# Biases on the rows' last channel, shorter clearing, four first projections in four banks, four weights fetched earlier

## The chip, the core and the metric

The kernel runs on one core of a Trainium2 chip. The metric is the device time of one launch in microseconds (us). The kernel before took 3951.41 us, the median of three runs (3949.12 to 3953.07). Its profiled execution took 3948.97 us, of which 3947.2 us lie between its first and its last instruction.

## The reference

The input `u` is 4 x 1024 rows (4096 tokens) of 256 channels, all in f32. Layer 0 adds to it the output of a state-space recurrence and of a mixture of 64 experts (six of them per token). Layer 1, cut to what matters:

```
xn = layernorm(x)                       # over the 256 channels, no scale or shift
Q, K, V = xn @ Wq + bq, xn @ Wk + bk, xn @ Wv + bv       # each 1024 = 16 heads x 64
scores[t,h,i,j] = Q[t,h,i] * K[t,h,j] / 8,  j <= i       # a 64 x 64 triangle per token and head
attn[t,h,i] = sum_j softmax_j(scores)[i,j] * V[t,h,j]
x = x + attn @ Wo + bo + (silu(xn @ wg') * (xn @ wu')) @ wd'   # wg', wu', wd': int32 / 127
```

The normalised row `xn` is the only input of the five projections (`Wq`, `Wk`, `Wv`, `wg`, `wu`). Its channels sum to zero.

## The kernel before, in words

The program runs in stages, each a `Block` in which the five engines run their own instruction lists and after which they meet at a barrier. Before the change's first place come normalisation, routing and the recurrence.

**Experts** (`routed_experts`). 256 blocks of 128 rows run in 32 turns of 8. SyncE's queue (SP) fetches in `turn_in` three weights, four row blocks, five weights and four row blocks per turn. A weight is fetched only where the block's expert is another than the last one. TensorE computes, ScalarE and VectorE evaluate, GpSimd's queue scatters the results to DRAM.

**Combine** (`combine`). For each of 32 tiles of 128 tokens SP loads six expert rows per token (768 KB, a ring of five buffers), TensorE sums five of them and VectorE one (`own_choices`), VectorE measures and normalises, TensorE transposes, ScalarE copies and stores the transposed tile `xT`. Behind the first five loads SP also fetches all weights of layer 1: `Wq`, `Wk`, `Wv`, `Wo`, the three integer weights into `stage`, and the three biases, each repeated over 128 partitions, into `rest`. VectorE's `weights(step)`, spread over every second tile from tile 9 on, splits the f32 biases into three bf16 parts on rows of `k.bias` (rows 0, 64 and 96, picked by ones in `part_rows`) and converts the integer weights.

**Attention and feed-forward** (`attention_and_ffn`). A first `Block` clears buffers: GpSimd the tails of `q` and `m` and the four `pv` buffers, VectorE the six `s` buffers, each over its whole width of 2240 or 2496 elements. Then the second `Block` runs 32 tiles of 24 chunks each (`NCH`). One chunk holds four key rows of the score triangle or rectangle, up to 128x2048 elements. It goes through these engines:

- VectorE `products` multiplies q by k (at_s, L1195/L1196),
- GpSimd subtracts a bound of the maximum, `m` (at_s, L1276),
- ScalarE takes the exponential (at_s, L1355),
- TensorE adds it to the denominators (`sum_den`, at_den, L1509),
- VectorE `times_v` multiplies by v (at_pv), three chunks later,
- TensorE adds that to the numerators (`sum_num`, at_num).

Between the chunks, at fixed chunk numbers, stands the preparation of the next half tile. `project` computes one of six projections per tile, 128x512 each: K halves 0 and 1 of the next tile at chunks 4 and 8, V half 1 at chunk 11, Q half 0 of the next tile at 17, V half 0 at 19, Q half 1 at 22. All share one PSUM bank, `work`, so each waits until ScalarE has copied the one before out of it. Behind K come two scans of VectorE (L1419, L1422) and ScalarE's `keep_k`. Behind Q comes `keep_q` (three copies, the last is `fall`), and then GpSimd's `maxima`, whose first step (L1256) waits for `fall`. Behind V comes `keep_v`; `show_v` (at_vp, L1330) gives v to VectorE at chunks 1 and 17. On ScalarE, chunk 0 is followed by `keep_q` of Q half 1, then by the exponential of chunk 1, then by `show_v`.

The order on every engine is written out by hand, in the tables `prepare`, `KEEP_...`, `SCAN`, `MAXIMA_...`. Ahead of the loop stand five projections for tile 0.

Of the kernel before, what the change touches and what calls it, by code (L numbers as in the profile page):

```python
# [13 lines left out]
P = 128  # L14
# [16 lines left out]
HID = 768  # L31
# [605 lines left out]
def routed_experts(nc, k, io, scratch):  # L637
# [3 lines left out]
    with ExitStack() as ctx:  # L641
# [21 lines left out]
        w_in, x_in, y_out = ([a.sem(f"{s}{j}") for j in range(RING)] for s in ("w_in", "x_in", "y_out"))  # L663

# [10 lines left out]
        with nc.Block() as block:  # L675
# [183 lines left out]
            def _(sp):  # L859
# [25 lines left out]

                for i in range(TURNS):
                    turn_in(i)


def combine(nc, k, io, scratch):  # L890
    with ExitStack() as ctx:
# [10 lines left out]
        rest = a.sb("rest", [P, 3 * HC])  # L902
# [7 lines left out]
        members = lambda g: slice(g * GROUP, (g + 1) * GROUP)  # L910
        with nc.Block() as block:
# [11 lines left out]
            def _(dve):  # L923
# [8 lines left out]
                parts = k.bias[:].rearrange("p w n -> p (w n)")  # L932

                def weights(step):

                    if step == 0:
                        dve.wait_ge(w_in, 160)
                        c.mark(v.memset(k.keep_max[:], 0.0))
                        c.mark(v.memset(k.keep_min[:], 0.0))
                        c.mark(v.memset(k.part_rows[:], 0.0))  # L940
                        c.mark(v.tensor_copy(parts, rest[:]))
                    elif step == 1:
# [3 lines left out]
                        for row in (0, 64, 96):  # L946
                            c.mark(v.memset(k.part_rows[row:row + 1, :], 1.0))
# [18 lines left out]
                def normalise(g):  # L966
                    dve.wait_ge(pow_done, g + 1)
                    for n in range(g * GROUP, (g + 1) * GROUP):
                        v.tensor_scalar(xn[:, n, :], k.x[:, n, :], mv[:, n, 0:1], rstd[:, n:n + 1],
                                        ALU.subtract, ALU.mult).then_inc(xn_done, 1)  # L970
# [26 lines left out]
            def _(pe):  # L997
                for n in range(NT + AFTER):
# [40 lines left out]
            def _(sp):  # L1039
# [13 lines left out]
                for i, name in enumerate(("WqT", "WkT", "WvT")):  # L1053
                    sp.dma_start(k.wqkv[i][:], io[name].rearrange("(c p) n -> p c n", p=P)).then_inc(w_in, 16)
                for i, name in enumerate(("bq", "bk", "bv")):
# [647 lines left out]
```

## Time and profile before

| | |
|---|---|
| three runs, median | 3951.41 us |
| profiled execution | 3948.97 us, span 3947.2 us |
| TensorE matmul busy | 3548.3 us (90%) |
| GpSimd busy | 3342.6 us (85%) |
| VectorE busy | 3260.5 us (83%) |
| ScalarE busy | 1973.2 us (50%) |
| experts, from about 384 to 830 us | 446 us |
| combine, from about 834 to 958 us | 124 us |
| attention and feed-forward, from about 961 us | 2986 us |

Busy time is counted per engine; idle time of an engine is attributed to what it waited for. A matmul in f32 appears as two records. TensorE's clock has two levels, 1.2 and 2.4 GHz; a granted clock of 1.00 is the upper one and 0.50 the lower one. A share of 0.98 in a stretch is a mean over both.

### The profile page before, as it was taken

The numbers are of one execution on the slowest core, as the hardware profiler recorded it, in microseconds if no ns is written. First come the engines' busy times: TensorE is split into PE (matmuls) and PEld (weight loads), VectorE is DVE, ScalarE is ACT, GpSimd is POOL, SyncE is SP. The second block draws the span as 40 slices with busy tenths as digits, with TensorE's granted clock in tenths as the row PEclk, the third lists the DMA queues.
The fourth block names the chain that finished last, engine by engine and source line by source line (L and its number), as shares of the span: only waits on it lengthen the run. The fifth ranks groups of instructions, "written<-read, shape, count | busy, mean of one in ns | idle before, by whom it ended". The sixth has DMA issues, their size and how long they took to land.

```text
span 3947.2 us, 72250 instructions
## 1 busy us (share of the span) xinstructions
PE 3548.3 (90%) x25960; PEld 3110.3 (79%) x26155; DVE 3260.5 (83%) x3712; ACT 1973.2 (50%) x2535; POOL 3342.6 (85%) x1498
## 2 busy tenths in 40 slices
PE   5594999966899999999999999999999999999999
PEld 4253888854688888888888888888888888888888
DVE  8332666647798899999999999899999999999988
ACT  1010333334555555555555655565555566555555
POOL 1675665622899999999999999999999999999997
PEclk8797999987999999999999999999999999999999
DMA  9323565676000000000000000000000000000000
GB/s 380 125 104 123 172 184 178 188 266 236 3 5 5 5 5 5 5 5 5 5 6 6 8 5 5 5 5 5 5 5 6 5 7 5 6 7 5 5 5 5
DMA packets 110635, 209.30 MB, mean 53 GB/s; under 512 B 16610, under 2 KB 77282, under 8 KB 110306
## 3 DMA queue, kind: packets, MB, share of 16 engines
q1 hardware_dynamic: 84192, 140.90, 11.2%
q0 software_dynamic: 21504, 59.93, 4.0%
q8 instruction: 192, 3.15, 0.3%
q10 hardware_dynamic: 4608, 4.20, 0.3%
q14 instruction: 139, 1.12, 0.1%
HBM read 183.34 MB, written 107.74 MB: 74 GB/s over the span
## 4 chain that ended last, share of the span: by engine, by line
POOL 37%; PE 18%; issue 15%; DVE 3%; ACT 1%; another core or an unknown queue 0%; POOLq 0%; DVEq 0%; ACTq 0%
POOL at_s L1276 34%; PE at_num L1509 7%; PE at_den L1509 6%; PE at_work L1487 3%; POOL at_m L1261 1%; POOL at_fall L1258 1%; PE at_work L1497 1%; DVE at_pv L1195 1%; DVE at_k_low L1422 1%; PE at_misc L1541 1%; PE at_misc L1535 1%; ACT at_s L1355 1%; DVE at_s L1195 1%; POOL at_m L1256 0%; DVE at_k_top L1419 0%
## 5 line engine op out<-in xcount | busy, mean ns | idle before, releaser
L1276 POOL TENSOR_TENSOR at_s<-at_s,at_m 128x2048 f32<-128x2048 f32 (+7 forms) x768 | 2511.1, 3305 | 32.6 <-DVE at_s L1195 24.5
L1355 ACT ACTIVATE at_s<-at_s 128x2048 f32<-128x2048 f32 (+7 forms) x768 | 1080.5, 1418 | 610.2 <-POOL at_s L1276 609.9
L1509 PE MATMUL at_den<-k_ident,at_s 128*128 128x128 f32 x9216 | 1135.2, 273 | 53.3 <-ACT at_s L1355 53.2
L1509 PE MATMUL at_num<-k_ident,at_pv 128*128 128x128 f32 x9216 | 1141.7, 274 | 15.8 <-issue 5.6
L1509 PEld LDWEIGHTS at_num<-k_ident,at_pv 128*128 128x128 f32 x9216 | 1048.0, 142 | 92.1 <-issue 70.3
L1509 PEld LDWEIGHTS at_den<-k_ident,at_s 128*128 128x128 f32 x9216 | 1037.0, 141 | 85.0 <-ACT at_s L1355 61.0
L1196 DVE TENSOR_TENSOR at_pv<-at_s,at_vp 128x2048 f32<-128x2048 f32 (+7 forms) x512 | 688.7, 1345 | 226.2 <-ACT at_vp L1330 179.9
L1196 DVE TENSOR_TENSOR at_s<-at_q,at_kp 128x2048 f32<-128x2048 f32 (+7 forms) x512 | 687.9, 1344 | 13.7 <-ACT at_kp L1325 10.0
L1195 DVE TENSOR_TENSOR at_pv<-at_s,at_vp 128x2048 f32<-128x2048 f32 x256 | 582.7, 2276 | 0.0
L1195 DVE TENSOR_TENSOR at_s<-at_q,at_kp 128x2048 f32<-128x2048 f32 x256 | 580.1, 2266 | 0.0
L1487 PE MATMUL at_work<-k_region,at_xT 128*128 128x512 f32 x788 | 406.0, 641 | 105.9 <-ACT at_k_far L1296 82.2
L692 POOL DMA_INDIRECT picked<-moe_yo,moe_row x256 | 270.5, 1057 | 183.0 <-DVE moe_row L786 124.4
L1487 PEld LDWEIGHTS at_work<-k_region,at_xT 128*128 128x128 f32 x788 | 140.0, 198 | 219.5 <-issue 101.3
L140 POOL DMA_INDIRECT slot_x<-s_xn,s_slot x192 | 190.9, 994 | 140.2 <-DMA slot_x<-k_region 76.4
L714 PE MATMUL moe_gu<-moe_xT,moe_w 128*128 128x128 f32 x2048 | 276.5, 278 | 5.9 <-DVE moe_xT L836 5.7
L714 PEld LDWEIGHTS moe_gu<-moe_xT,moe_w 128*128 128x128 f32 x2048 | 250.5, 193 | 15.0 <-DVE moe_xT L836 13.8
L753 ACT ACTIVATE moe_gate<-moe_gu 128x128 f32<-128x128 f32 x256 | 71.0, 277 | 294.4 <-PE moe_gu L714 293.6
L1296 ACT COPY at_k_near<-at_work 128x256 f32<-128x256 f32 x66 | 24.6, 372 | 348.0 <-DVE at_k_low L1422 348.0
L1497 PE MATMUL at_work<-at_xT,k_region 128*128 128x128 f32 x1536 | 187.2, 275 | 0.0
L830 DVE TENSOR_TENSOR moe_hid<-moe_gate,moe_gu 128x128 f32<-128x128 f32 x256 | 73.2, 286 | 133.1 <-ACT moe_gate L753 128.3
L1497 PEld LDWEIGHTS at_work<-at_xT,k_region 128*128 128x128 f32 x1536 | 179.1, 192 | 0.0
L1256 POOL TENSOR_TENSOR at_m<-at_k_top,at_m 128x512 f32<-128x512 f32 x65 | 101.2, 1557 | 86.5 <-ACT at_fall L1310 85.7
(232 smaller groups left out, 3396.6 us busy)
## 6 DMA issues: line engine op xcount, KB each, us to landing
moe_w<-experts SPq DMA_DIRECT2D x256, 384.0 KB
slot_x<-k_region SPq DMA_DIRECT2D x16, 2144.0 KB, 25.4
moe_x<-slot_x SPq DMA_DIRECT2D x256, 134.0 KB, 2.3
cmb_y<-picked SPq DMA_DIRECT2D x32, 768.0 KB, 7.5
at_xT<-xT SPq DMA_DIRECT2D x33, 128.0 KB, 2.0
e_x<-u SPq DMA_DIRECT2D x4, 1024.0 KB, 9.3
picked<-moe_yo,moe_row POOLq DMA_INDIRECT x256, 3.1
xT<-cmb_xT ACTq DMA_DIRECT2D x32, 128.0 KB, 5.0
```

Of the source, the lines that this page charges most:

```text
L140: nc.gpsimd.indirect_dma_start(scratch["slot_x"], bass.IndirectOffsetOnAxis(ap=k.slot[:, n, j:j + 1], axis=0), k.xn[:, n, :], None).then_i ...
L692: pool.indirect_dma_start(scratch["picked"], bass.IndirectOffsetOnAxis(ap=row[i % 2][:, j:j + 1], axis=0), yo[j][:], None).then_inc(y_out[ ...
L714: ins = nc.tensor.matmul(gu[j % 2][:, s, :], w[j][:, (2 * s + c) * P:(2 * s + c + 1) * P], xT[j][:, c, :], start=(c == 0), stop=(c == DC - 1))
L830: nc.vector.tensor_tensor(hid[j][:], gate[j][:], gu[j % 2][:, 1, :], ALU.mult).then_inc(hid_ready, 1)
L1195: return nc.vector.tensor_tensor(by_row(out), by_row(other), keys, ALU.mult)
L1196: return nc.vector.tensor_tensor(out, other, keys, ALU.mult)
L1256: nc.gpsimd.tensor_tensor(rows(m[h]), turned(k_top), rows(m[h]), ALU.mult).then_inc(max_step, 1)
L1276: nc.gpsimd.tensor_tensor(part(s_slot, c), part(s_slot, c), by_query(m[unit_of(c)][:], c), ALU.subtract).then_inc(sub_done, 1)
L1355: nc.scalar.activation(part(s_slot, c), part(s_slot, c), ACT.Exp, scale=C ** -0.5).then_inc(exp_done, 1)
L1487: nc.tensor.matmul(work[:], xT[u][:, c, :], wqkv[which][:, c, cols], start=(c == 0), stop=False)
L1497: ins = nc.tensor.matmul(work[:, (2 * s + h) * P:(2 * s + h + 1) * P], w[:, c, tile * P:(tile + 1) * P], xT[u][:, c, :], start=(c == 0), s ...
L1509: ins = nc.tensor.matmul(dst[:, b * P:(b + 1) * P], buf[:, at:at + P], k.ident[:], start=(c in (0, NTRI) and x == 0 and b == 0), stop=Fals ...
```

## The change

The last channel (number 255) of every normalised row is set to 1.0 instead of its value. Since the channels sum to zero, the value there is minus the sum of the other 255, so the projections stay what they were if the last row of each weight is subtracted from all rows. The last row itself then becomes free and takes the bias (and zero for `wg` and `wu`).

- Projection: two f32 matmuls instead of two f32 matmuls and one bf16 matmul.
- Combine: GpSimd writes the ones once, VectorE normalises 255 columns, the `weights` steps subtract the last rows (`last`, `last_up`, fetched repeated over the partitions) from `Wq`, `Wk`, `Wv` (128x2048 each) and from the two integer weights (128x1536 each). SP waits for `shifted` and writes the three biases (4 KB each) over the last rows.
- `Wq`, `Wk`, `Wv` and `Wo` are fetched in the experts' stage, behind turns 6, 12, 18 and 24.
- The clearing `Block` is gone. Each engine clears at the head of the main `Block`, and of each `s` and `pv` buffer only the prefixes of its four rows (48 or 112 elements each).
- The first four projections go to four banks (`work`, `misc`, `num[1]`, `den[1]`), with no wait between them.

```diff
@@ routed_experts, SP @@
+                late = ((k.wqkv[0], "WqT"), (k.wqkv[1], "WkT"), (k.wqkv[2], "WvT"), (k.wo, "Wo"))
                 for i in range(TURNS):
                     turn_in(i)
+                    if i in (6, 12, 18, 24):
+                        dst, name = late[i // 6 - 1]
+                        sp.dma_start(dst[:], io[name].rearrange("(c p) n -> p c n", p=P)).then_inc(late_in, 16)
+                sp.wait_ge(late_in, 16 * len(late))
@@ combine @@
+                nc.gpsimd.memset(view(xn[:], [[D, NT]], D - 1), 1.0).then_inc(ones_set, 1)
...
-                        c.mark(v.memset(k.part_rows[:], 0.0))
-                        c.mark(v.tensor_copy(parts, rest[:]))
...
-                        c.mark(v.tensor_tensor(rest[:], rest[:], parts, ALU.subtract))
-                    elif step == 2:
-                        c(v.tensor_copy(parts[64:128, :], rest[64:128, :]))
-                    elif step == 3:
-                        c(v.tensor_tensor(rest[64:128, :], rest[64:128, :], parts[64:128, :], ALU.subtract))
-                    elif step == 4:
-                        c(v.tensor_copy(parts[96:128, :], rest[96:128, :]))
+                    if step < 3:
+                        w = k.wqkv[step]
+                        v.tensor_tensor(w[:], w[:], view(last[:], [[0, DC], [1, HC]], step * HC), ALU.subtract
+                                        ).then_inc(shifted, 1)
+                    elif step < 5:
+                        s = stage[step - 3][:].rearrange("p (c n) -> p c n", c=DC)
+                        c(v.tensor_tensor(s, s, view(last_up[:], [[0, DC], [1, HID]], (step - 3) * HID), ALU.subtract))
...
+                sp.wait_ge(shifted, 3)
+                for i, name in enumerate(("bq", "bk", "bv")):
+                    sp.dma_start(k.wqkv[i][P - 1:P, DC - 1, :], io[name].rearrange("(o n) -> o n", o=1)).then_inc(bias_in, 16)
@@ attention_and_ffn @@
-                for t in s_slot:
-                    nc.vector.memset(t[:], 0.0).then_inc(zeroed, 1)
+                for i in range(S_RING):
+                    v.memset(lead(s_slot, i), 0.0).then_inc(zeroed, 1)
...
-                        nc.tensor.matmul(work[:], xT[u][:, c, :], wqkv[which][:, c, cols], start=(c == 0), stop=False)
-                    nc.tensor.matmul(work[:], part_rows[:], bias[:, which, cols], start=False, stop=True
-                                     ).then_inc(work_done, 1)
+                        ins = nc.tensor.matmul(bank[:], xT[u][:, c, :], wqkv[which][:, c, cols], start=(c == 0),
+                                               stop=(c == DC - 1))
+                    ins.then_inc(work_done, 1)
...
                 project(0, 0, 1, 0)
+                project(0, 0, 1, 1, misc)
+                project(0, 0, 0, 0, num[1])
+                project(0, 0, 2, 0, den[1])
                 pe.wait_ge(k_out, 1)
-                project(0, 0, 1, 1)
-                pe.wait_ge(k_out, 2)
-                project(0, 0, 0, 0)
-                pe.wait_ge(q_out, 1)
-                project(0, 0, 2, 0)
+                project(0, 0, 0, 1)
                 pe.wait_ge(v_out, 1)
-                project(0, 0, 0, 1)
```

On TensorE, at the head of attention, stand before (L1487 is a projection's f32 matmul, L1488 its bias matmul, L1509 a sum of a chunk; at_work is the shared bank):

```order
L1487 MATMUL at_work<-k_region,at_xT 128x512 x2
L1488 MATMUL at_work<-k_bias,k_part_rows 128x512
L1487 MATMUL at_work<-k_region,at_xT 128x512 x2
L1488 MATMUL at_work<-k_bias,k_part_rows 128x512
L1487 MATMUL at_work<-k_region,at_xT 128x512 x2
L1488 MATMUL at_work<-k_bias,k_part_rows 128x512
L1487 MATMUL at_work<-k_region,at_xT 128x512 x2
L1488 MATMUL at_work<-k_bias,k_part_rows 128x512
L1487 MATMUL at_work<-k_region,at_xT 128x512 x2
L1488 MATMUL at_work<-k_bias,k_part_rows 128x512
L1509 MATMUL at_den<-k_ident,at_s 128x128 x20
```

And now, at the same place (L1492 and L1514 are the same two lines in the changed file):

```order
L1492 MATMUL at_work<-k_region,at_xT 128x512 x2
L1492 MATMUL at_misc<-k_region,at_xT 128x512 x2
L1492 MATMUL at_num<-k_region,at_xT 128x512 x2
L1492 MATMUL at_den<-k_region,at_xT 128x512 x2
L1492 MATMUL at_work<-k_region,at_xT 128x512 x2
L1514 MATMUL at_den<-k_ident,at_s 128x128 x20
```

Five bias matmuls are gone, and four of the five projections have a bank of their own. In the tile loop each projection loses its bias matmul in the same way and nothing else moves.

On SP's queue, at the head of combine, stand before (cmb_y is the ring of expert rows):

```order
L1044 DMA cmb_y<-picked 128x1536 x5
L1052 DMA cmb_bo<-bo 128x256
L1054 DMA k_region<-WqT 128x2x1024
L1054 DMA k_region<-WkT 128x2x1024
L1054 DMA k_region<-WvT 128x2x1024
L1056 DMA cmb_rest<-bq 128x1024
L1056 DMA cmb_rest<-bk 128x1024
L1056 DMA cmb_rest<-bv 128x1024
L1057 DMA k_region<-Wo 128x8x256
L1059 DMA cmb_stage<-wgT 128x2x768
L1059 DMA cmb_stage<-wuT 128x2x768
L1059 DMA cmb_stage<-wdT 128x6x256
```

And now, at the same place:

```order
L1049 DMA cmb_y<-picked 128x1536 x5
L1057 DMA cmb_bo<-bo 128x256
L1059 DMA cmb_last<-WqT 128x1024
L1059 DMA cmb_last<-WkT 128x1024
L1059 DMA cmb_last<-WvT 128x1024
L1061 DMA cmb_last_up<-wgT 128x768
L1061 DMA cmb_last_up<-wuT 128x768
L1063 DMA cmb_stage<-wgT 128x2x768
L1063 DMA cmb_stage<-wuT 128x2x768
L1063 DMA cmb_stage<-wdT 128x6x256
L1049 DMA cmb_y<-picked 128x1536 x8
```

Four weights and three repeated biases have left this place, five repeated last rows have come.

On SP's queue behind the experts' turn 6 stands now (before, the second row is not there; turns 12, 18 and 24 have `WkT`, `WvT` and `Wo` in its place):

```order
L868 DMA moe_x<-slot_x 128x268 x4
L892 DMA k_region<-WqT 128x2x1024
L873 TENSOR_LOAD c_fetch
L873 ISA x2
L874 ISA
L874 DMA moe_w<-experts 128x768
```

The weight has come between the last row blocks of one turn and the first expert weight of the next.

## Rows read from the trace of the kernel before

**Rows 1.** Windows: us, busy us (instructions) per engine, granted clock, DMA share, GB/s.
```profile
384.00:830.00 446.00, 410.97 (x3044) 364.35 (x3042) 293.19 (x1145) 164.88 (x509) 270.47 (x256) 1.00 0.59 180
...
834.40:958.50 124.10, 87.84 (x384) 72.37 (x384) 78.10 (x184) 61.78 (x192) 15.01 (x16) 0.83 0.92 334
...
863.10:876.90 13.80, 4.83 (x16) 4.04 (x17) 2.56 (x7) 0.94 (x4) 0.00 (x0) 0.57 1.03 406
...
1103.70:3846.90 2743.20, 2616.38 (x20275) 2358.53 (x20453) 2529.77 (x1771) 1591.10 (x1620) 2657.72 (x931) 0.99 0.02 6
```
**Rows 2.** Windows of two single tiles, the same columns (PE, PEld, DVE, ACT, POOL).
```profile
1195.00:1286.80 91.80, 87.48 (x677) 78.67 (x682) 84.31 (x60) 53.15 (x55) 88.49 (x32) 0.98 0.02 6
...
2385.20:2475.40 90.20, 86.14 (x678) 78.17 (x683) 84.40 (x60) 52.95 (x55) 88.73 (x33) 1.00 0.02 6
```
**Rows 3.** Groups of GpSimd, 1103.7 to 3846.9 us: busy, mean ns, idle before and releasers.
```profile
L1276 POOL TENSOR_TENSOR at_s<-at_s,at_m 128x768 f32<-128x768 f32 (+1 forms) x721 | 2356.1, 3302 | 30.3 <-DVE at_s L1195 23.7 <-POOL at_m L1261 3.6 <-DVE at_s L1196 1.3
L1256 POOL TENSOR_TENSOR at_m<-at_k_top,at_m 128x512 f32<-128x512 f32 x60 | 93.5, 1558 | 55.2 <-ACT at_fall L1310 54.5
```
**Rows 4.** Timeline of GpSimd: start, us, what, idle before it and its releaser.
```profile
1926.45 1.54 POOL L1256 TENSOR_TENSOR at_m<-at_k_top,at_m 128x512 f32<-128x512 f32 x1 [0.82 <-ACT at_fall L1310]
...
1970.81 4.57 POOL L1276 TENSOR_TENSOR at_s<-at_s,at_m 128x2048 f32<-128x2048 f32 x1 [0.65 <-DVE at_s L1195]
...
2001.32 1.56 POOL L1256 TENSOR_TENSOR at_m<-at_k_top,at_m 128x512 f32<-128x512 f32 x1 [1.48 <-ACT at_fall L1310]
...
2464.76 8.64 POOL L1276 TENSOR_TENSOR at_s<-at_s,at_m 128x2048 f32<-128x2048 f32 x3 [0.17 <-DVE at_s L1196]
2473.89 1.54 POOL L1256 TENSOR_TENSOR at_m<-at_k_top,at_m 128x512 f32<-128x512 f32 x1 [0.49 <-ACT at_fall L1310]
```
**Rows 5.** Timeline of ScalarE and VectorE around the hand-over of Q half 1 and v.
```profile
1924.80 0.58 ACT L1306 COPY at_q<-at_work 128x512 f32<-128x512 f32 x1 [1.30 <-remote]
...
2473.68 0.43 ACT L1355 ACTIVATE at_s<-at_s 128x256 f32<-128x256 f32 x1
...
1927.25 2.29 DVE L1196 TENSOR_TENSOR at_pv<-at_s,at_vp 128x2048 f32<-128x2048 f32 x1 [5.61 <-ACT at_vp L1330]
```
**Rows 6.** Timeline of TensorE, matmuls (PE) and weight loads (PEld), around two projections.
```profile
1940.34 1.88 PE L1487 MATMUL at_work<-k_region,at_xT 128*128 128x512 f32 x4
1942.27 1.04 PE L1509 MATMUL at_num<-k_ident,at_pv 128*128 128x128 f32 x8
...
1969.28 2.43 PE L1487 MATMUL at_work<-k_region,at_xT 128*128 128x512 f32 x4 [2.41 <-ACT at_k_far L1296]
...
1941.20 0.19 PEld L1487 LDWEIGHTS at_work<-k_region,at_xT 128*128 128x128 f32 x1 [0.24 <-issue]
1941.63 0.10 PEld L1488 LDWEIGHTS at_work<-k_bias,k_part_rows 128*128 128x128 bf16 x1 [0.24 <-issue]
```
**Rows 7.** Timeline of four engines at the start of attention.
```profile
973.90 2.14 DVE L1211 MEMSET at_s<- 128x2496 f32 x1 [0.47 <-issue]
...
976.53 0.83 SPq L1223 DMA_DIRECT2D at_xT<-xT  x2
...
978.54 3.78 PE L1487 MATMUL at_work<-k_region,at_xT 128*128 128x512 f32 x4 [21.36 <-DMA at_xT<-xT]
...
983.92 1.19 DVE L1422 TENSOR_TENSOR_SCAN at_k_low<-k_region,at_work 128x512 f32<-128x512 f32 x1
...
961.07 0.24 POOL L1203 MEMSET at_q<- 128x64 f32 x2 [7.14 <-POOLq L911]
...
1004.89 8.60 POOL L1276 TENSOR_TENSOR at_s<-at_s,at_m 128x2048 f32<-128x2048 f32 x3 [1.43 <-DVE at_s L1196]
```
**Rows 8.** Timeline of TensorE in combine, its first sum behind the weights' transfers.
```profile
872.07 8.17 PE L1004 MATMUL cmb_acc<-cmb_y,cmb_diag 128*128 128x256 f32 x30 [19.61 <-DMA cmb_y<-picked]
```
**Rows 9.** Timeline in the experts: SP's queue, then TensorE.
```profile
593.64 1.77 SPq L867 DMA_DIRECT2D moe_x<-slot_x  x4
...
597.81 0.43 PE L705 MATMUL moe_tr<-k_ident,moe_x 128*128 128x128 f32 x2 [0.73 <-DMA moe_x<-slot_x]
```

More of the change, by code:

```diff
@@ L901, in combine @@
         stage = [a.sb(f"stage{i}", [P, DC * HID], I32) for i in range(3)]
-        rest = a.sb("rest", [P, 3 * HC])
+        last = a.sb("last", [P, 3, HC])
+        last_up = a.sb("last_up", [P, 2, HID], I32)
+        shifted, bias_in, ones_set = a.sem("shifted"), a.sem("bias_in"), a.sem("ones_set")
         tr = [a.ps(f"tr{j}", [P, DC, P]) for j in range(2)]
@@ L1283, in tile @@
                             gated(t)
+                for x in (q[0], q[1], m[0], m[1]):
+                    nc.gpsimd.memset(x[:, HALF:QL], 0.0).then_inc(padded, 1)
+                for i in range(PV_RING):
+                    nc.gpsimd.memset(lead(pv_slot, i), 0.0).then_inc(padded, 1)
+                pool.wait_ge(padded, 4 + PV_RING)
                 for step in range(3):
@@ L1290, in _, with keep_k @@
             def _(act):
-                def keep_k(t, u, half):
+                def keep_k(t, u, half, bank=work):
                     act.wait_ge(scanned, t * 4 + (half * 2 + 2))
@@ L1305, in keep_q, with keep_v @@
                     wait(act, mult_done, past)
-                    nc.scalar.copy(q[h][:, 0:HALF], work[:])
+                    nc.scalar.copy(q[h][:, 0:HALF], bank[:])
                     wait(act, sub_done, past)
-                    nc.scalar.activation(m[h][:, 0:HALF], work[:], ACT.Relu)
+                    nc.scalar.activation(m[h][:, 0:HALF], bank[:], ACT.Relu)
                     wait(act, max_step, n * 3)
-                    nc.scalar.activation(fall[:], work[:], ACT.Relu, scale=-1.0).then_inc(q_out, 1)
-                def keep_v(n, use):
+                    nc.scalar.activation(fall[:], bank[:], ACT.Relu, scale=-1.0).then_inc(q_out, 1)
+                def keep_v(n, use, bank=work):
                     act.wait_ge(work_done, use)
                     wait(act, vp_ready, n)
-                    nc.scalar.copy(vv[:], work[:]).then_inc(v_out, 1)
+                    nc.scalar.copy(vv[:], bank[:]).then_inc(v_out, 1)
                 def keep_up(t, r, use):
@@ L1410, in times_v, with scan @@
                     multiply(part(pv_slot, c), part(s_slot, c), by_key(vp[:], c), c).then_inc(pv_done, 1)
-                def scan(t, half, step, use):
+                def scan(t, half, step, use, bank=work):
                     flat = lambda x: x[:].rearrange("p h c -> p (h c)")
@@ L1468, in tile @@
                             output(t - 1)
+                for i in range(S_RING):
+                    v.memset(lead(s_slot, i), 0.0).then_inc(zeroed, 1)
                 for half in range(2):
                     for step in range(2):
-                        scan(0, half, step, half + 1)
+                        scan(0, half, step, half + 1, (work, misc)[half])
+                dve.wait_ge(zeroed, S_RING)
+                dve.wait_ge(padded, 4 + PV_RING)
                 tile_loop(dve, tile)
@@ L1481, in _, with project @@
             def _(pe):
-                def project(t, u, which, half):
+                def project(t, u, which, half, bank=work):
                     pe.wait_ge(xT_in[u], 8 * (t - u) + 16)
@@ L1630, in lay_out_shared @@
     k.wqkv = [wq, wk, wv]
-    k.bias, k.part_rows = a.sb("bias", [P, 3, HC], BF16), a.sb("part_rows", [P, P], BF16)
 def build(nc, io, scratch):
```

47 lines of the change are left out of this document (19 added, 28 removed).

## The prediction, written before the changed kernel ran

> **What bounds the kernel now.** I read the windows first, to see in which stage the time lies. Of 3947.2 us, 2743.2 are thirty tiles of attention, 91.44 us each [rows 1]. There GpSimd is busy for 2657.7 us, 88.6 per tile, and TensorE for 2616.4. So GpSimd is the busiest engine, and 88.6 us is a floor that no part of this change moves. The groups of GpSimd [rows 3] tell what stands above the floor: its first maximum step waited 54.5 us for ScalarE's `fall` copy and its subtractions 25.0 us for VectorE's products, together with small waits 85 us in thirty tiles.
>
> The two single tiles show that there are two kinds [rows 2]. One takes 91.8 us at a mean clock of 0.98, the other 90.2 us at 1.00. A mean of 0.98 is one stretch at the lower level. Of the thirty windows from 1103.7 us on, 22 are of the first kind and 8 of the second. GpSimd works 88.5 and 88.7 us in them, so the 1.6 us between them is idle time of GpSimd that TensorE's clock causes.
>
> The timeline of GpSimd shows where it waits [rows 4]. In a tile with the drop: 1.48 us for `fall` of Q half 0 (at 2001.32), 0.82 for `fall` of Q half 1 (at 1926.45) and 0.65 for VectorE at chunk 12 (at 1970.81). In a tile without: 0.49 for Q half 1, none for Q half 0.
>
> Following these back gives a ring. ScalarE waited 1.30 us for the projection Q half 1 ("remote" is its PSUM bank) and then shows v. VectorE starts on it at 1927.25 after 5.61 us idle [rows 5], and works without a pause until its K scan, behind which V half 1 starts at 1969.28, after 2.41 us in which TensorE idled [rows 6]. From there TensorE works without a pause through V half 1, Q half 0, V half 0 to Q half 1. So per tile VectorE's part and TensorE's part follow each other, and four bias matmuls lie in TensorE's part. The other two (K halves) lie beside VectorE's part and only lengthen TensorE's idle time.
>
> **Part 1, the bias matmuls (33 us gained).** Four records of a projection stand 0.43 us apart (weight loads at 1941.20 and 1941.63), so they take 1.72. From the first of them to the next sum are 1942.27 - 1940.34 = 1.93 us [rows 6]. The bias matmul is the rest, 0.21 us at the upper clock, 0.42 at the lower.
>
> - Tile with a drop: four of them leave the ring, one at the lower clock (V half 1 took 2.43 instead of 1.88 us and begins at the drop). 3 x 0.21 + 0.42 = 1.05, I take 1.0. Such a tile goes to 90.8. GpSimd does not stop this: of its 3.3 us of waiting (91.8 - 88.5), the two for `fall` shrink.
> - Tile without: the four give 0.85, but ScalarE has the exponential of chunk 1 ahead of `show_v`. It began at 2473.68 [rows 5], and GpSimd had finished chunk 1 at 2464.76 + 8.64 = 2473.40 [rows 4]. So only 0.28 us can be gained there before ScalarE waits for GpSimd instead. Behind that GpSimd's own path is late next. I take 0.25; the tile goes to 89.9. The bounds are 0.25 and 0.49, what GpSimd waits for `fall`.
>
> How many tiles keep the drop is not in the rows. The idle time that goes with it, 2.41 us, becomes about 0.2 longer (K half 1 loses its bias too), but the tile gets another length and the drop has been missing in tiles with the same wait. I take half. Then a tile is 90.35 on the mean, 1.09 less than 91.44, and for 30.5 tiles (tile 0 has no such waits, the last has half) 33 us. All tiles with the drop: 0.64 x 30.5 = 20. None: 1.54 x 30.5 = 47. The share as today (22 of 30): 90.56, 27.
>
> **Part 2, the clearing (15.4 us gained).** The last clearing of VectorE ended at 976.04 and SP issued the first `xT` load at 976.53, while the stage had begun at 961.07 on GpSimd [rows 7]. Without the barrier the load is issued at about 961.1. The small clearings are hidden: six on VectorE, at most a fifth of the elements of the old ones, before its first scan, which waits for the load (978.54 - 976.53 = 2.0 us) and the first projection (3.8 us); GpSimd's before its first maximum, much later still.
>
> **Part 3, four banks (11 us gained).** From the first projection at 978.54 to GpSimd's first subtraction at 1004.89 are 26.35 us [rows 7]. The projections ran at the lower clock (four records in 3.78 us, 0.86 apart). In a row, without biases, four take 13.8 us at that clock and 0.2 to end, so V is there at 992.5 in the old times. Copying v and showing k take 0.6 each and the product 2.3 [rows 5], the hand-over 0.2: the subtraction starts at 996.2, 8.7 us earlier. If the clock rises after K half 0, V is there at about 987.3, but then the K scans and ScalarE's copies are late next: scan of K half 0 at 982.1, of half 1 until 986.7 (four scans of 1.19 us [rows 7]), ScalarE's two copies of k in 0.7 (an estimate, half as wide as the 0.6 us copies), three of q in 1.6, v and k in 1.1, product 2.3 and hand-overs, giving 993.4, which is 11.5 earlier. In combine TensorE resumed at 872.07 [rows 8], and the mean clock of 863.1 to 876.9 was 0.57 [rows 1], which is 1.9 us at the upper level: it rose 2.9 us after the work resumed. So I expect it to rise during the first projections, and take 11; bounds 8.6 and 12. The Trainium skill, "TensorE: Matmul & The Clock Gate", section "Part 1: The HAM clock gate (the "warmup" mystery)", says that the throttled state is the default and activity releases it; by that rule, to which this row agrees, the value is 11.5, and if it did not hold here, 8.7.
>
> **Part 4, combine (9 us gained).** The stage is bound by its transfers: 0.92 busy, 334 GB/s over 124 us, with VectorE at 78 us of 124 [rows 1]. TensorE waited 19.61 us for the sixth load behind the weights [rows 8]. By the shapes of the queue's rows, out go 4 x 1024 + 3 x 512 = 5632 KB, in come 3 x 512 + 2 x 384 = 2304 KB. The difference is 3328 KB or 3.41 MB: 8.4 us at the 406 GB/s of the wait, 10.2 at the stage's 334. I take 9, with bounds 7 and 12. The Trainium skill, "DMA: Bandwidth & Descriptors", section "Specifications", gives a limit of about 358 GB/s from HBM per core; the row of 406 is above it, and by the page the term would be 9.5. VectorE's new steps are three of 128x2048 (2.29 each by the product of that size [rows 5]) and two of 128x1536 (an estimate of 1.7 each), 10.3 us in place of as many steps over 3072 columns, so they are costed at nothing; they stand beside the loads. If that cover were gone they cost part of their 10.3, which the lower bound of 7 allows for. TensorE's new wait for the ones ends before its first data. SP's wait for `shifted` stands behind the last load; queued behind it are the last three stores, and the shifts are done by tile 13.
>
> **Part 5, the experts (7 us lost).** Four transfers of 1.05 MB, 2.6 us each at 406 GB/s, come between turns. Behind each stand the next three expert weights and the row blocks, whose first was issued at 593.64 and for which TensorE already waited 0.73 us at 597.81 [rows 9]. The transfer engines are busy 0.59 of this stage [rows 1], so some of each is absorbed in the 7 us between. I take 1.75 each, 7 in all; bounds 0, and 4 x (2.6 + 0.5 for issuing) = 12.4.
>
> **Sum.** 33 + 15.4 + 11 + 9 - 7 = 61.4. The profiled execution took 3948.97 us: 3887.6. It is 2.4 below the median of the runs, by which the sum gives 3890. I predict 3889.
>
> **Rivals.**
> - The drop comes in every tile, because TensorE idles longer before V half 1. For it: the idle time grows. Against: 8 of 30 tiles escape with about the same wait. Part 1 gives 20: 3902.
> - The drop is gone, since the tile's length changes. Part 1 gives 47: 3875.
> - GpSimd is the bound and the loop gains nothing. For it: 88.6 of 91.4 us busy, by far the fullest. Against: its waits end with ScalarE, and those with TensorE. Part 1 gives 0: 3922.
> - Slower: with less work TensorE falls to the lower clock more than once per tile, also in the pause around chunk 8. The price of a drop is 1.6 us per tile. Parts 2 to 5 give 28.4 us, so it decides from two drops in every tile (90.8 + 1.6 = 92.4, 0.96 x 30.5 = 29 lost), and three give 3999. Against: TensorE works 87.5 of 91.8 us. The Trainium skill, "TensorE: Matmul & The Clock Gate", section "HAM oscillation — how this bites in real kernels", says a loop with pauses for data can be throttled anew in each round; the trace agrees that one does so in 22 tiles of 30.
>
> **How the numbers follow.** Forecast 56%, drop in every tile 17%, drop gone 15%, no gain in the loop 9%, slower 2%, and 1% that the parts cancel. The forecast's own terms, with all at their bounds, span 3874 to 3903. The range reaches to the two rivals beside it and their bounds: 3864 to 3917. A change of 0.2% (7.9 us) is about what a measurement of this kernel tells from none. Faster by more 0.97, within it 0.01, slower 0.02.
>
> **What the changed profile would show.** Tiles of 89.9 and 90.8 us, at clocks of 1.00 and 0.98; GpSimd's wait for `fall` down from 54.5 to below 25 us in thirty tiles. First `xT` load within 1 us of the stage's start; the first subtraction about 17 us behind the load, not 28. TensorE's long wait in combine near 11 us instead of 19.6. In the experts four waits for row blocks 1 to 3 us longer than now. Wrong would be: tiles still at 91.4, or an experts' stage longer by over 12 us.

## The result: 3863 us, 2.2% less than before

The changed kernel takes 3862.6 us (median of four runs, 3861.58 to 3867.46), the kernel before beside it 3951.64 (3949.12 to 3953.07). The ratio is 0.9778, with a 95% interval of 0.9761 to 0.9795. That is 89 us gained, where 61 were forecast, and 1.4 us below the end of the range (3864). The direction, the ring of engines and the two parts at the start of attention were right. The step that failed is the bound on what a tile without a drop of the clock can gain: 0.25 us was forecast, 0.84 came. Combine's term was too small as well.

The profiled execution took 3861.88 us. The head of its page:

```profile
span 3860.1 us, 72041 instructions
PE 3497.0 (91%) x25958; PEld 3084.9 (80%) x25958; DVE 3241.8 (84%) x3708; ACT 1971.6 (51%) x2535; POOL 3336.4 (86%) x1499
```

GpSimd's own work is nearly what it was (3336 against 3343 us; the 6 us are its shorter clearing). Of the 87.1 us by which the span is shorter, 81 are waiting of GpSimd. They fall into four stretches, each read between two marks that both traces have:

| stretch, us | before | after | gain | forecast |
|---|---|---|---|---|
| start to the first load of expert rows (end of the experts) | 834.39 | 837.46 | -3.1 | -7 |
| from there to the start of the attention stage (combine) | 126.7 | 114.1 | 12.6 | 9 |
| stage start to GpSimd's first subtraction | 43.8 | 17.3 | 26.5 | 26.4 |
| first subtraction to the end (the loop) | 2942.3 | 2891.3 | 51.0 | 33 |

So the start of attention came out as worked out, and the miss is the loop (18 us), combine (3.6) and the experts (3.9).

Windows of the changed kernel, to be held beside [rows 1, 2]: us, then busy us (instructions) of PE, PEld, DVE, ACT and POOL, the granted clock, DMA share and GB/s. The last three are consecutive tiles, cut where GpSimd begins chunk 1.

```profile
384.00:833.00 449.00, 413.45 (x3040) 364.93 (x3038) 293.26 (x1146) 165.10 (x509) 270.89 (x256) 0.99 0.61 188
837.50:951.50 114.00, 85.39 (x384) 69.76 (x384) 75.39 (x180) 61.80 (x192) 15.53 (x17) 0.89 0.93 339
880.00:920.00 40.00, 35.31 (x168) 28.69 (x167) 38.39 (x83) 27.18 (x84) 8.20 (x6) 1.00 1.01 359
...
2409.40:2499.70 90.30, 86.12 (x674) 78.03 (x673) 84.34 (x59) 53.03 (x54) 88.58 (x33) 0.98 0.02 6
2499.70:2589.70 90.00, 85.82 (x682) 78.13 (x681) 84.08 (x59) 53.02 (x54) 88.63 (x33) 1.00 0.02 6
2589.70:2679.00 89.30, 85.12 (x678) 77.54 (x677) 84.08 (x59) 53.02 (x54) 88.61 (x33) 1.00 0.02 6
```

This pattern of three repeats through most of the loop: a tile with the clock's drop (0.98 on the mean), the one behind it, which still pays for it at its head, and a clean one of 89.3. The second to the thirty-first tile, from 1057.5 to 3752.6 us, take 89.84 us each, against 91.41 before (1093.5 to 3835.9). 11 of these 30 have a drop, before 22 of 30. All counts of drops below are of the same thirty tiles.

The groups of GpSimd in the loop (busy, mean ns | idle before and releasers) answer to [rows 3]:

```profile
L1272 POOL TENSOR_TENSOR at_s<-at_s,at_m 128x768 f32<-128x768 f32 (+1 forms) x720 | 2354.4, 3305 | 22.6 <-DVE at_s L1203 14.3 <-DVE at_s L1204 3.0 <-POOL at_m L1257 2.0
L1252 POOL TENSOR_TENSOR at_m<-at_k_top,at_m 128x512 f32<-128x512 f32 x60 | 93.6, 1560 | 15.8 <-ACT at_fall L1311 14.1
```

The wait for `fall` went from 54.5 to 14.1 us (below 25 was expected) and that for VectorE from 25.0 to 17.3.

Here is the start of attention in the timeline of the changed kernel (start, us, engine, line, what, idle before it), to be held beside [rows 7]:

```profile
951.56 0.84 SPq L1219 DMA_DIRECT2D at_xT<-xT  x2
951.67 2.06 DVE L1472 MEMSET at_s<- 128x192 f32 x6 [4.68 <-PEq L920]
953.60 3.78 PE L1492 MATMUL at_work<-k_region,at_xT 128*128 128x512 f32 x4 [5.94 <-DMA at_xT<-xT]
957.18 2.54 PE L1492 MATMUL at_misc<-k_region,at_xT 128*128 128x512 f32 x4
959.56 1.88 PE L1492 MATMUL at_num<-k_region,at_xT 128*128 128x512 f32 x4
961.28 1.88 PE L1492 MATMUL at_den<-k_region,at_xT 128*128 128x512 f32 x4
...
964.43 1.52 POOL L1252 TENSOR_TENSOR at_m<-at_k_top,at_m 128x512 f32<-128x512 f32 x1 [11.23 <-ACT at_fall L1311]
...
968.85 4.50 POOL L1272 TENSOR_TENSOR at_s<-at_s,at_m 128x2048 f32<-128x2048 f32 x1
```

The load goes out at the stage's start. The projections follow each other without a gap; the first ran at the lower clock (3.78 us), the second partly, the others at the upper (1.88). The first subtraction stands 17.3 us behind the load.

### The profile page after: what moved, and what is told of

Its sections match the earlier page's. It is cut to its first block, busy times and chain, and to the rows that moved or that the text cites. A ratio compares the mean times of both kernels' runs of the same rounds, so it can differ in the third digit from the quotient of the medians.

```text
span 3860.1 us, 72041 instructions
## 1 busy us (share of the span) xinstructions
PE 3497.0 (91%) x25958; PEld 3084.9 (80%) x25958; DVE 3241.8 (84%) x3708; ACT 1971.6 (51%) x2535; POOL 3336.4 (86%) x1499
## 4 chain that ended last, share of the span: by engine, by line
PE 53%; DVE 13%; issue 8%; ACT 1%; DVEq 0%; POOL 0%; ACTq 0%; DMA 0%; POOLq 0%
PE at_num L1514 20%; PE at_den L1514 18%; PE at_work L1492 8%; DVE at_s L1203 5%; PE at_work L1502 4%; DVE at_pv L1203 4%; PE at_misc L1540 2%; DVE at_k_low L1423 2%; PE at_misc L1546 1%; DVE at_k_top L1420 1%; DVE at_pv L1204 1%; ACT at_k_far L1297 0%; ACT at_s L1356 0%; DVEq L49 0%; DVEq L1407 0%
## 5 line engine op out<-in xcount | busy, mean ns | idle before, releaser
L1514 PE MATMUL at_den<-k_ident,at_s 128*128 128x128 f32 x9216 | 1136.1, 273 | 64.0 <-ACT at_s L1356 63.9
L1514 PE MATMUL at_num<-k_ident,at_pv 128*128 128x128 f32 x9216 | 1141.1, 274 | 0.5 <-DVE at_pv L1204 0.5
L1514 PEld LDWEIGHTS at_num<-k_ident,at_pv 128*128 128x128 f32 x9216 | 1047.1, 142 | 107.0 <-issue 96.2
L1514 PEld LDWEIGHTS at_den<-k_ident,at_s 128*128 128x128 f32 x9216 | 1037.9, 141 | 95.8 <-ACT at_s L1356 59.5
L1492 PE MATMUL at_work<-k_region,at_xT 128*128 128x512 f32 x776 | 378.7, 611 | 87.3 <-ACT at_k_far L1297 81.4
L1492 PEld LDWEIGHTS at_work<-k_region,at_xT 128*128 128x128 f32 x776 | 133.9, 192 | 190.2 <-issue 94.9
L706 PE MATMUL moe_tr<-k_ident,moe_x 128*128 128x128 f32 x512 | 101.0, 280 | 62.9 <-DMA moe_x<-slot_x 62.6
```

The lines of the kernel that those rows point to most:

```text
L706: ins = nc.tensor.transpose(tr[j % 2][:, c, :], xr[:, j, c * P:(c + 1) * P], k.ident[:])
L1492: ins = nc.tensor.matmul(bank[:], xT[u][:, c, :], wqkv[which][:, c, cols], start=(c == 0), stop=(c == DC - 1))
L1514: ins = nc.tensor.matmul(dst[:, b * P:(b + 1) * P], buf[:, at:at + P], k.ident[:], start=(c in (0, NTRI) and x == 0 and b == 0), stop=Fals ...
```

## The experiments

Each was run with the kernel before on the same chip; the ratios are against that. The stretches of e1 to e8 are compared with the changed kernel's trace. Times are compared with the changed kernel's median, which is of another round: the kernel before took 3951.6 us beside it, 3946.6 beside e1 to e4, 3951.2 beside e5 to e8 and 3947.3 beside e9 to e11. So a difference of up to 5 us between two medians tells nothing without a trace.

**e1_add_k and e2_add_vq: which bias matmuls were worth something.** A bf16 matmul on zeros takes the place of the bias matmul in the loop, in e1 only behind the two K projections, in e2 only behind the V and Q projections.

```
+                    if more:      # e1: which == 1 (K); e2: which != 1 (V, Q)
+                        ins = nc.tensor.matmul(bank[:], zb[:, 0:P], zb[:], start=False, stop=True)
```

> The changed kernel with one bf16 128x512 matmul of zeros put back into the two K projections of each tile (62 in all, 0.21 us each, 13 us of TensorE). Theory A (ring: TensorE's part runs from V half 1 to Q half 1, VectorE's part from v to the K scan): the K projections lie beside VectorE's part, so only TensorE's idle time before V half 1 shrinks, from 2.6 to about 2.4 us, and the time stays within 6 us of the changed kernel, 3857 to 3869. Rival B (TensorE's total work sets the loop): 13 us more, 3876.

> The changed kernel with the same matmul of zeros put back into the four V and Q projections of each tile instead (27 us of TensorE). Theory A: these lie in TensorE's part of the ring, so nearly the whole gain in the loop goes: tiles of 90.1 to 91.8 us again, mean about 91.2, 3863 + 42 = 3905. Rival B: 27 us more, 3890.

Measured: e1 3861.98 us (ratio 0.9784, 0.9768 to 0.9801), its loop 2890.0 us with 10 drops, where the changed kernel has 2891.3 and 11. e2 3913.7 us (0.9916, 0.9899 to 0.9932), its loop 2943.8 us with 25 drops. Two windows of e2, a single tile and then most of the loop, and its wait for `fall`:

```profile
2252.90:2344.70 91.80, 87.62 (x681) 78.88 (x681) 84.31 (x60) 53.05 (x54) 88.52 (x32) 0.98 0.02 6
1103.70:3757.10 2653.40, 2532.69 (x19706) 2275.86 (x19705) 2444.38 (x1710) 1538.26 (x1567) 2567.43 (x900) 0.98 0.02 6
...
L1253 POOL TENSOR_TENSOR at_m<-at_k_top,at_m 128x512 f32<-128x512 f32 x59 | 91.8, 1557 | 58.1 <-ACT at_fall L1312 57.7
```

The whole of the loop's gain is back out, with the old tile length and the old wait. So the ring of the prediction stands: two matmuls per tile beside VectorE's part are free, four in TensorE's part cost 1.7 us per tile, twice their own 0.85 [rows 6]. The other half fits the drops, which come back with them: 14 more, at 1.7 us each (see below), are 24 of the 52 us.

**e3_fill: the price of the drops.** Ten bf16 matmuls on zeros stand in TensorE's idle time ahead of V half 1.

```
+                        for _ in range(10):
+                            nc.tensor.matmul(den[1][:], zb[:, 0:P], zb[:], start=False, stop=False, ...)
```

> The changed kernel with ten bf16 matmuls of zeros (2.1 us) into the running denominator bank just ahead of V half 1's wait in each tile, where TensorE idles 2.6 us. Theory A: idle time of 0.5 us, no drop of the clock in any tile, all tiles about 89.3 us instead of 89.9 on the mean: 3863 - 18 = 3845. Rival B (the loop is set by TensorE's total work): 31 x 2.1 = 66 us more, 3929. Rival C (the drop has no price for the loop): unchanged, 3863.

Measured: 3849.63 us (0.9754, 0.9738 to 0.9771), 13 less than the changed kernel. Windows of e3, the loop and one tile:

```profile
1103.70:3757.10 2653.40, 2593.87 (x20396) 2332.33 (x20394) 2495.23 (x1753) 1577.82 (x1611) 2630.42 (x924) 1.00 0.02 6
2323.60:2412.80 89.20, 87.18 (x688) 78.39 (x686) 84.08 (x60) 52.94 (x55) 88.50 (x31) 1.00 0.02 6
```

The clock is 1.00 over the loop, 27 of 30 tiles take 89.2 to 89.4 us, and one drop is left of 11. The loop is 14.3 us shorter, 1.4 per drop. TensorE did more work, and the kernel became faster.

**e4_v_first: what bounds the clean tile.** `show_v` goes ahead of the exponential of chunk 0 on ScalarE; before it stood behind that exponential, three copies and the exponential of chunk 1.

```
-                SHOW_V, SHOW_K_FAR, SHOW_K_NEXT = {1: 0, 17: 1}, 13, 21
+                SHOW_V, SHOW_K_FAR, SHOW_K_NEXT = {17: 1}, 13, 21
+                        if c == 0:
+                            show_v(t, 0)
```

> The changed kernel with show_v of each tile's first half ahead of the exponential of chunk 0 on ScalarE, instead of behind the Q copies and the exponential of chunk 1. Theory A (the ring runs through ScalarE's exponential, its three Q copies and show_v to VectorE): VectorE's first product with v starts when the exponential of chunk 0 is there, about 2.5 us earlier, the idle times of TensorE and GpSimd go, tiles fall to GpSimd's 88.6 to 88.8 us, 3863 - 35 = 3828. Rival B (TensorE's total work is the bound): no gain, 3863. Rival C (ScalarE waits for GpSimd's chunk 1 there, as the prediction had it): 0.3 us per tile, 3853.

Measured: 3830.63 us (0.9711, 0.9695 to 0.9727), 32 less than the changed kernel. Its loop and one tile in windows:

```profile
1103.70:3757.10 2653.40, 2553.36 (x20190) 2317.38 (x20189) 2518.20 (x1765) 1590.87 (x1618) 2643.67 (x929) 1.00 0.02 6
2490.70:2579.50 88.80, 85.34 (x679) 77.53 (x678) 84.26 (x59) 53.19 (x56) 88.55 (x33) 1.00 0.02 6
```

GpSimd is busy 88.55 of 88.8 us: with this edit the busiest engine binds. ScalarE's order was what held the clean tile of the changed kernel at 89.3. Three drops are left.

**e5_late_back: the price of fetching four weights in the experts.** The four transfers go back to combine, everything else stays.

```
-                    if i in (6, 12, 18, 24):
-                        ...
+                for dst, name in ((k.wqkv[0], "WqT"), (k.wqkv[1], "WkT"), (k.wqkv[2], "WvT"), (k.wo, "Wo")):
+                    sp.dma_start(...)
```

> The changed kernel with Wq, Wk, Wv and Wo fetched at the head of combine again, ahead of the last rows. Theory A (combine is bound by its transfers): the experts end 3.1 us earlier, TensorE waits for the sixth expert rows 4.2 MB / 0.406 = 10.3 us longer, net 7 us slower than the changed kernel, 3870. Rival B (the weights were hidden in combine anyway): 3 us faster, 3860.

Measured: 3863.46 us (0.9779, 0.9761 to 0.9796), the same as the changed kernel. TensorE's sums in e5's combine, behind the loads:

```profile
831.89 12.89 PE L1005 MATMUL cmb_acc<-cmb_y,cmb_diag 128*128 128x256 f32 x50 [14.92 <-DMA cmb_y<-picked]
867.08 9.76 PE L1005 MATMUL cmb_acc<-cmb_y,cmb_diag 128*128 128x256 f32 x30 [22.30 <-DMA cmb_y<-picked]
```

And the same two rows of the changed kernel:

```profile
841.68 13.10 PE L1009 MATMUL cmb_acc<-cmb_y,cmb_diag 128*128 128x256 f32 x50 [14.79 <-DMA cmb_y<-picked]
865.86 8.65 PE L1009 MATMUL cmb_acc<-cmb_y,cmb_diag 128*128 128x256 f32 x30 [11.08 <-DMA cmb_y<-picked]
```

The wait for the sixth load doubles from 11.08 to 22.30 us and combine is 13.5 us longer, but the experts end 9.9 us earlier. The experts' end scatters, so one pair of traces doesn't price it. From TensorE's first transposition to its last output in the experts, the four traces with no weights among the experts' loads took 446.4, 444.0, 444.2 and 439.4 us, the eight with them 447.1 to 452.1: on the mean 443.5 and 449.7, a price of 6.2 us. By the medians, moving the four transfers was worth 1 us, less than can be told from none: this part of the change is not shown to have gained anything.

**e6_clear_block: the clearing.** The clearing `Block` of before stands ahead of the main one again.

```
+        with nc.Block() as block:      # GpSimd the four pv, VectorE the six s buffers, whole width
+            ...
+                for t in s_slot:
+                    nc.vector.memset(t[:], 0.0).then_inc(wide[1], 1)
```

> The changed kernel with a Block ahead of attention that clears the whole s and pv buffers again. The first xT load is issued 15.4 us later and all behind it: 3863 + 15 = 3878. Rival (part of it is given back, since TensorE's clock and the first tiles absorb it): under 10 us.

Measured: 3878.04 us (0.9814, 0.9796 to 0.9831), 15.4 more than the changed kernel, as worked out. The trace of e6:

```profile
956.87 8.10 POOL L1216 MEMSET at_pv<- 128x2240 f32 x4 [7.12 <-ACTq L1211]
957.40 1.93 DVE L1222 MEMSET at_s<- 128x2240 f32 x1 [4.99 <-PEq L920]
...
969.69 2.14 DVE L1222 MEMSET at_s<- 128x2496 f32 x1 [0.47 <-issue]
972.32 0.84 SPq L1234 DMA_DIRECT2D at_xT<-xT  x2
```

The first load waits for the last clearing again. The stage begins with GpSimd's clearing at 956.87, 15.4 us ahead of the load. (Combine itself was 3 us longer in this trace, which the medians don't show.)

**e7_one_bank: the first projections.** They go through `work` one by one again, each behind its wait, without biases.

```
-                project(0, 0, 1, 1, misc)
-                project(0, 0, 0, 0, num[1])
-                project(0, 0, 2, 0, den[1])
                 pe.wait_ge(k_out, 1)
+                project(0, 0, 1, 1)
+                pe.wait_ge(k_out, 2)
+                ...
```

> The changed kernel with the first four projections one after the other in one bank, each waiting for ScalarE's copy (without bias matmuls). From the first projection to GpSimd's first subtraction 24 to 25 us instead of 15.2: 3863 + 9.5 = 3872. Rival (the three-fold wait was hidden by the K scans): under 4 us.

Measured: 3868.38 us (0.9789, 0.9772 to 0.9807), 5.8 more than the changed kernel. From the first projection to the first subtraction are 24.59 us in its trace instead of 15.25, 9.3 more; the intervals don't exclude either. TensorE in e7:

```profile
955.62 3.70 PE L1492 MATMUL at_work<-k_region,at_xT 128*128 128x512 f32 x4 [6.10 <-DMA at_xT<-xT]
962.42 3.68 PE L1492 MATMUL at_work<-k_region,at_xT 128*128 128x512 f32 x4 [3.10 <-ACT at_k_far L1297]
969.20 3.68 PE L1492 MATMUL at_work<-k_region,at_xT 128*128 128x512 f32 x4 [3.10 <-ACT at_k_far L1297]
974.54 1.98 PE L1492 MATMUL at_work<-k_region,at_xT 128*128 128x512 f32 x4 [1.66 <-ACT at_fall L1311]
```

With waits of 3.10 us between them three projections run at the lower clock (3.7 us); without waits only the first does (3.78 us). Part of what four banks gain is the clock. Of the two rivals, 9.5 by the waits and under 4, the trace agrees with the first, and the medians lie between them.

**e8_vector_pad: does VectorE bind combine?** Four more VectorE instructions stand beside the weight steps 1 to 4.

```
+                    if step in (1, 2, 3, 4):
+                        c(v.tensor_tensor(pad[:], last[:, 0, :], last[:, 1, :], ALU.subtract))
```

> The changed kernel with four more VectorE subtractions of 128x1024 (1.2 us each, 5 us in all) in combine's weight steps 1 to 4, their results unused. Theory A (in its middle combine is bound by VectorE, so the shorter weight steps gave the 3.3 us that the prediction costed at nothing): combine 4 to 5 us longer, 3867. Rival B (transfers bind it throughout): no change in combine.

Measured: 3866.81 us (0.9787, 0.977 to 0.9805). The four take 1.21, 1.21, 1.19 and 1.21 us, 4.8 in all, and combine is 3.4 us longer. The middle of combine in e8, in one window:

```profile
880.00:920.00 40.00, 32.51 (x147) 26.28 (x146) 39.14 (x79) 23.44 (x73) 9.80 (x6) 0.96 0.96 318
```

VectorE is busy 39.1 of 40 us here and 38.4 in the changed kernel, and the stage does less in the same time: 318 GB/s against 359. That speaks for VectorE being late there, not the transfers, with 0.7 of each microsecond given to it coming out at the end. It isn't shown: the medians are 4.2 us apart, but the runs of the two kernels overlap, and combine took 113.3 to 117.0 us in the eight traces with the same weight steps and early weights but without the four instructions. The 0.7 is an estimate.

**e9_before_v_first and e10_before_fill: the same two edits on the kernel before.** e9 is the edit of e4 made to the kernel before, e10 that of e3. Both keep all bias matmuls.

> The kernel before (with all its bias matmuls) with show_v of each tile's first half ahead of the exponential of chunk 0. Theory A (the ring TensorE, ScalarE's copies, show_v, VectorE set the loop, not TensorE's work): the ring is cut, tiles go to 88.7 to 89.5 us in spite of the bias matmuls, 3949 - 70 = 3879. Rival B (TensorE's total work with the bias matmuls, 86 to 87.5 us per tile and its waits, is the bound): tiles stay above 90.5, 3920 or more.

> The kernel before with ten bf16 matmuls of zeros into the denominator bank ahead of V half 1's wait, where TensorE idles. Theory A (a drop costs the tile 1.6 us): no drops, all tiles 90.1 us instead of 91.8 in 22 of 30, 3949 - 37 = 3912. Rival (2.1 us more work in TensorE's part): unchanged or slower.

Measured: e9 3870.77 us (0.9807, 0.9789 to 0.9826), its loop 2866.2 us with one drop and most tiles at 88.8 to 88.9 us. e10 3902.95 us (0.9884, 0.9866 to 0.9903), its loop 2901.9 us with none. Most of the loop in one window, e9 and then e10:

```profile
1103.70:3757.10 2653.40, 2566.76 (x20151) 2327.94 (x20328) 2523.55 (x1759) 1583.41 (x1608) 2639.04 (x923) 1.00 0.02 6
...
1103.70:3757.10 2653.40, 2596.06 (x20182) 2325.26 (x20357) 2484.65 (x1738) 1550.06 (x1583) 2609.53 (x911) 1.00 0.02 6
```

Nearly all tiles of e10 take 90.1 to 90.2 us, the clean tile of before [rows 2]. So the ring has two cures that need no change of the biases: a shorter path through ScalarE (e9) takes 76 us out of the loop of the kernel before, and keeping the clock up (e10) takes out 40 (22 drops fewer, 1.8 us each).

Held beside e4 and e3, these two also tell what the biases themselves are worth. With the clock kept up, taking them out shortens the loop from 2901.9 us (e10) to 2877.0 (e3), 0.84 us per tile from 90.13 to 89.29 where neither has a drop: four matmuls of 0.21, nothing more. With `show_v` first it shortens the loop only from 2866.2 (e9) to 2858.8 (e4), 7 us. The 51 us of the changed kernel's loop were the price of the same matmuls at one particular order of ScalarE.

**e11_v_first_pieces: a version that beats both.** The edit of e4, and the four early weights in sixteen pieces of 256 KB, one behind each of the turns 6 to 21.

```
-                    if i in (6, 12, 18, 24):
+                    if 6 <= i < 6 + len(pieces):
+                        dst, src = pieces[i - 6]
```

> The changed kernel with show_v first, and the four early weights cut into 16 pieces of 256 KB, one behind each of the experts' turns 6 to 21. If each whole weight stalls TensorE because 2.6 us of transfers stand ahead of the next row blocks, pieces of 0.65 us are absorbed by the idle transfer engines: the experts end 3 us earlier than with whole weights, 3831 - 3 = 3828. Rival (the bytes and the issuing cost, not their lump): the same 3831 or slower.

Measured: 3828.73 us (0.9699, 0.9681 to 0.9717), the fastest, 34 less than the changed kernel. It can't be told from e4 (3830.63). Its profiled run was the quickest of its four (3819.85 us; the others 3828.5 to 3829.0). In it the experts took 441.8 us, as without any weights, so that one trace speaks for the pieces, the medians for no more than 2 us.

## Why the prediction was too high

**Part 1, no-drop tile: the step that failed.** The prediction let such a tile gain 0.25 us, with 0.49 as the most, because GpSimd had finished chunk 1 at 2473.40 and ScalarE would then wait for it. That time was the end of a row of three merged instructions, taken for the end of chunk 1 [rows 4]. The three are chunks 0, 1 and 2. A narrower view of GpSimd has chunk 1 by itself, and ScalarE's own rows in the kernel before, which the prediction did not use, tell what it waited for:

```profile
2469.26 0.73 POOL L1276 TENSOR_TENSOR at_s<-at_s,at_m 128x256 f32<-128x256 f32 x1
...
2469.35 1.91 ACT L1355 ACTIVATE at_s<-at_s 128x2048 f32<-128x2048 f32 x1 [4.69 <-POOL at_s L1276]
2472.24 0.58 ACT L1306 COPY at_q<-at_work 128x512 f32<-128x512 f32 x1 [0.98 <-remote]
2472.72 0.60 ACT L1308 ACTIVATE at_m<-at_work 128x512 f32<-128x512 f32 x1
2473.21 0.61 ACT L1310 ACTIVATE at_fall<-at_work 128x512 f32<-128x512 f32 x1
...
2474.51 1.50 ACT L1355 ACTIVATE at_s<-at_s 128x1536 f32<-128x1536 f32 x1
```

The exponential of chunk 0 (2048 columns) began at 2469.35, when the first of the three subtractions had ended. The next two are 256 and 1536 columns wide: chunks 1 and 2. GpSimd finished chunk 1 at 2469.99, 3.7 us before ScalarE took it up at 2473.68 [rows 5]. Nothing of GpSimd stood in the way. What could be gained is ScalarE's wait for the projection, 0.98 us. A clean tile of the changed kernel shows it used up:

```profile
2589.77 1.91 ACT L1356 ACTIVATE at_s<-at_s 128x2048 f32<-128x2048 f32 x1 [5.13 <-POOL at_s L1272]
2591.78 0.59 ACT L1307 COPY at_q<-at_work 128x512 f32<-128x512 f32 x1
2592.26 0.60 ACT L1309 ACTIVATE at_m<-at_work 128x512 f32<-128x512 f32 x1
2592.75 0.60 ACT L1311 ACTIVATE at_fall<-at_work 128x512 f32<-128x512 f32 x1
2593.22 0.43 ACT L1356 ACTIVATE at_s<-at_s 128x256 f32<-128x256 f32 x1
2593.53 0.61 ACT L1331 COPY at_vp<-at_v 128x512 f32<-128x512 f32 x1
```

ScalarE now works from the exponential of chunk 0 to `show_v` without a pause, and it begins when GpSimd hands over chunk 0. The clean tile went from 90.12 (90.13 in e10's thirty) to 89.28, 0.84 us instead of 0.25: all of the 0.85 us of four bias matmuls, which the prediction had worked out and then capped. Its upper bound of 0.49, GpSimd's wait for `fall`, failed too, since GpSimd's waits for VectorE shrank as well. e4 shows by taking `show_v` out of this row that the row is what binds the changed kernel's clean tile. Over 30.5 tiles the term was 19 us too small (89.9 forecast, 89.28 measured).

**Part 1, the drops.** I took half the tiles at a price of 0.9 us (90.8 against 89.9). It was 11 of 30, and one drop costs 1.7 us, since the tile behind pays as well: 90.3 + 90.0 + 89.3 is 1.7 more than three clean tiles. That is 0.62 us per tile where I had 0.45, 5 us more cost, which hid a quarter of the first error. Of the remaining 4 us of the loop's 18, 3 are its end: from the last tile's first subtraction on the kernel became 3.7 us shorter, where half a tile's gain, 0.5, was counted. The rest is rounding.

Why it is every third tile isn't settled. The changed kernel's timeline of TensorE has the same idle time ahead of V half 1 in a tile with the drop (first row) and in the next one (second row):

```profile
2456.02 2.89 PE L1492 MATMUL at_work<-k_region,at_xT 128*128 128x512 f32 x4 [2.62 <-ACT at_k_far L1297]
...
2546.98 1.98 PE L1492 MATMUL at_work<-k_region,at_xT 128*128 128x512 f32 x4 [2.62 <-ACT at_k_far L1297]
```

The forecast had no rule for the share, and the experiments give none; e3 and e10 show only that work in that pause keeps the clock up. The Trainium skill, "TensorE: Matmul & The Clock Gate", section "HAM oscillation — how this bites in real kernels", describes a loop that is throttled anew in each round of waiting; here that holds for 11 rounds of 30 and not for the others, with an equal pause.

**Parts 2 and 3 were right.** The clearing gave 15.4 us (e6: 15.4 in the medians and in the trace). For the banks 11 were forecast, and 11.1 came from the first projection to the first subtraction against [rows 7]. e7 gives 9.3 of these to the banks by its trace and 5.8 by its median; the clock rose in the second projection, as the case of 11.5 had it.

**Part 4, combine: 12.6 for 9.** TensorE's long wait was 11.08 us, near 11 as expected, and the sixth tile was summed 9.3 us earlier against the first load. The other 3.3 came behind it, and their cause is only in part known. VectorE's weight steps were costed at nothing because the stage as a whole is bound by transfers. But between 880 and 920 us VectorE is busy 37.9 of 40 us in the kernel before and 38.4 in the changed one, and its steps became 2.4 us shorter: five subtractions of 2.23, 2.28, 2.27, 1.72 and 1.74 us in place of 12.6 us of casts, subtractions and clearings. Two of the five in the changed kernel, and then two of before's with its window (columns as above):

```profile
881.26 2.23 DVE L954 TENSOR_TENSOR k_region<-k_region,cmb_last 128x2048 f32<-128x2048 f32 x1
...
904.95 1.74 DVE L958 TENSOR_TENSOR cmb_stage<-cmb_stage,cmb_last_up 128x1536 int32<-128x1536 int32 x1
```

```profile
880.00:920.00 40.00, 34.02 (x153) 28.33 (x152) 37.89 (x79) 23.65 (x73) 7.17 (x6) 0.91 0.94 320
...
887.06 1.70 DVE L941 CAST k_bias<-cmb_rest 128x3072 bf16<-128x3072 f32 x1
...
894.77 3.36 DVE L948 TENSOR_TENSOR cmb_rest<-cmb_rest,k_bias 128x3072 f32<-128x3072 f32 x1
```

At e8's 0.7 that is 1.7 us, by estimate. The rest, 1.6 us, is left open. A rival that no run tests is TensorE's clock: it was 0.91 in that window before and 1.00 now. e5, too, moved combine by more than its bytes: 13.5 us for the four weights, where 10.3 were worked out.

**Part 5, the experts: -3.1 for -7.** By the one pair of profiles the term was twice too large, by the means over twelve kernels (6.2) it was about right. The pair's 3.1 fits the scatter of this stage, and it doesn't bear out the mechanism: the waits for row blocks behind the four transfers were 2.00, 1.08, 1.50 and 0.51 us, not 1 to 3 longer each, and over the whole stage they sum to 23.1 us, against 22.6 before. What grew in this pair is TensorE's busy time, from 410.97 [rows 1] to 413.45 us, at a clock of 0.99 instead of 1.00. The longest of the four waits, in the changed kernel:

```profile
478.34 0.43 PE L706 MATMUL moe_tr<-k_ident,moe_x 128*128 128x128 f32 x2 [2.00 <-DMA moe_x<-slot_x]
```

**The rivals.** The drop in every tile and the bound by GpSimd did not come. "The drop is gone" (47 us) was nearest to the 51 of the loop, but by luck: a third of the tiles keep the drop, and the clean tile gained more than it says. More than one drop per tile, the slower case, did not come either.

## What to carry to other kernels

- Work in a ring of engines is worth its own time, and more where a drop of the clock comes with it; the same work beside the ring is worth nothing (e2: 51 us, e1: 0). Its price holds for one order of the engines: with e4's edit all bias matmuls together are worth 7 us. Follow who waits for whom around a whole iteration before pricing an instruction, and look for an instruction that stands in the ring only by its place in an engine's order: moving one copy (e4) brought 32 us, for nothing removed.
- When a bound rests on when an engine finished a step, read that step's own row. A merged row gives the end of its last member; a narrower view shows a member by itself, and the widths of the consumer's rows tell which members they are.
- A stage that is bound by its transfers on the mean can have an engine nearly full in its middle (VectorE 37.9 of 40 us, in a stage where it works 78 of 124): look at windows inside the stage before something is costed at nothing.

## What the hardware showed unexpectedly

- Ten small matmuls on zeros in a pause of TensorE made the kernel 13 us faster (e3) and the kernel before 44 us faster (e10), by keeping the granted clock at 1.00.
- Equal pauses of 2.62 us before the same instruction, in consecutive tiles, once stood at a fall of the granted clock and once did not.
- The experts' stage of the same instructions took 439.4 to 446.4 us in four profiled executions, while the stretch from combine's first load to attention's first load took 142.0 to 142.4 us in the three of them that have the combine and the clearing of the kernel before. A term of a few us there can't be read from one pair of profiles.
